# Query tiles of the first batch through DRAM: attention and mixture layer, one core

## The reference, cut to what matters

```python
x = x + xattn(layernorm(x), ctx, ctx, q_norm_w, k_norm_w, w_out)   # x (4, 512, 512), ctx (4, 512, 128)
x = x + ffn(layernorm(x), ...)

def xattn(q, k, v, ...):                  # 16 query heads of width 32, 4 key heads, 4 query heads a key head
    q, k = rms_norm(q), rms_norm(k)
    q, k = rope(q), rope(k)
    scores = einsum(q, k) / sqrt(32), causal mask, softmax
    return (scores @ v).reshape(B, T, 512) @ w_out.T

def ffn(x, ...):                          # 128 experts as mixtures of 8 bases, top 4, and a shared part
    basis = silu(x @ w_gate) * (x @ w_up)                            # (tokens, 8, 256)
    mixed = per expert, basis weighed with mix(amplitudes); times w_down; summed with the router's weights
    return mixed + silu(x @ shared_gate) * (x @ shared_up) @ shared_down
```

## Time and profile before

| | us |
|---|---|
| median of 3 runs | 840.32 |
| lowest, highest | 839.88, 840.95 |
| profiled execution, first to last instruction | 839.9 |
| TensorE busy in it | 783.9 (93%) |
| VectorE, ScalarE, GpSimd busy | 664.1, 578.4, 525.0 |

### The profile page before, as it was taken

How to read it: one execution, slowest core, us unless ns; L and a number is a source line. 1 busy time by engine, 2 the same in 40 slices (tenths; PEclk the granted TensorE clock), 3 DMA queues, 4 the chain that set the end, 5 groups by cost and what they waited for, 6 DMA issues and landing times. The chain is left out here.

```text
span 839.9 us, 15209 instructions
## 1 busy us (share of the span) xinstructions
PE 783.9 (93%) x4180; PEld 610.7 (73%) x4180; DVE 664.1 (79%) x1635; ACT 578.4 (69%) x1413; POOL 525.0 (63%) x687
## 2 busy tenths in 40 slices
PE   3768899899999999989999999989999999999998
PEld 2645566677877777767777788767777787788876
DVE  7657678789888878889888878779878787688774
ACT  3867787677777767778777677678777775654542
POOL 5547457986488646997477834997566624661561
PEclk9969699999999999999999999999999999999999
DMA  8222144445445445744454435545445435454550
GB/s 300 104 68 80 28 130 166 142 143 168 155 161 170 149 156 174 230 144 129 147 192 161 153 119 182 168 143 174 148 162 169 152 114 173 158 184 130 205 192 26
DMA packets 57051, 127.02 MB, mean 151 GB/s; under 512 B 10920, under 2 KB 28040, under 8 KB 56968
## 3 DMA queue, kind: packets, MB, share of 16 engines
q1 hardware_dynamic: 56968, 126.04, 45.5%
HBM read 107.55 MB, written 4.46 MB: 133 GB/s over the span
## 5 line engine op out<-in xcount | busy, mean ns | idle before, releaser
L1602 PE MATMUL u<-w_h,t_h 128*128 128x512 f32 x640 | 258.9, 404 | 5.3 <-POOL w_l L889 2.7
L1259 DVE TENSOR_TENSOR w_l<-w_raw,w_h 128x512 fp32r<-128x512 f32 x288 | 253.4, 907 | 0.2 <-ACT w_h L931 0.2
L1602 PE MATMUL u<-w_l,t_h 128*128 128x512 f32 x640 | 251.2, 393 | 0.0
L1602 PE MATMUL u<-w_h,t_l 128*128 128x512 f32 x640 | 251.0, 392 | 0.0
L931 ACT ACTIVATE w_h<-w_raw 128x512 fp32r<-128x512 f32 x384 | 219.2, 621 | 13.4 <-DMA w_raw<-in_w_units 13.1
L889 POOL TENSOR_TENSOR w_l<-w_raw,w_h 128x512 fp32r<-128x512 f32 x96 | 138.2, 1440 | 98.3 <-ACT w_h L931 97.5
L965 ACT ACTIVATE scores<-scores,mx 128x384 f32<-128x384 f32 (+1 forms) x224 | 128.4, 573 | 78.3 <-DVE mx L1203 77.1
L1203 DVE CUSTOM_DVE_ANT_0 scores<-s,mask_qk 128x384 f32<-128x384 f32 (+1 forms) x224 | 112.3, 503 | 45.5 <-PE s L1480 44.8
L1602 PEld LDWEIGHTS u<-w_h,t_h 128*128 128x128 f32 x640 | 120.9, 189 | 33.7 <-issue 6.1
L897 POOL TENSOR_TENSOR macc<-macc,gb 128x256 f32<-128x256 f32 x112 | 103.5, 926 | 66.4 <-DVE gb L1360 66.0
L1602 PEld LDWEIGHTS u<-w_h,t_l 128*128 128x128 f32 x640 | 120.5, 188 | 27.1
(11 more groups left out here) (151 smaller groups left out, 1196.1 us busy)
## 6 DMA issues: line engine op xcount, KB each, us to landing
w_raw<-in_w_units SPq DMA_DIRECT2D x160, 512.0 KB, 4.2
w_raw<-in_w_out_t SPq DMA_DIRECT2D x16, 512.0 KB, 5.0
w_raw<-in_shared_w_down SPq DMA_DIRECT2D x16, 512.0 KB, 4.5
q_st<-turned_h SPq DMA_DIRECT2D x232, 32.0 KB, 1.9
out<-x SPq DMA_DIRECT2D x16, 256.0 KB, 2.2
q_st<-turned_l SPq DMA_DIRECT2D x116, 32.0 KB, 1.9
x<-in_x SPq DMA_DIRECT2D x3, 1024.0 KB, 8.9
k_st<-turned_h SPq DMA_DIRECT2D x48, 32.0 KB, 1.9
```

Source lines behind the costliest of these rows:

```text
L1259: e.tensor_tensor(w_l[:, i % WR, k, :], w_raw[:, i % WR, k, :], f32(w_h[:, i % WR, k, :]), ALU.subtract).then_inc(s_wl, 1)
L1602: last = e.matmul(u_bank[n % 2][:], t[:, k, cols], ww[:, i % WR, k, :], start=(k == 0 and m == 0), stop=(k == KC - 1 and m == 2))
```

## The change

Four more tiles are named in the tuple that selects the path through DRAM:

```diff
-THROUGH_DRAM = (5,)
+THROUGH_DRAM = (5, 6, 7, 8, 9)
```

## The result

| | before | after |
|---|---|---|
| median, us | 840.15 (4 runs) | 853.07 (851.58 to 853.58, 4 runs) |
| ratio to before | | 1.0140, 95% interval 1.0125 to 1.0156 |
| profiled execution, first to last instruction | 839.9 | 851.7 |

The changed kernel is 1.4% slower, about 11.8 us by the ratio. I forecast 848.8, with 851.8 as the upper end: the direction and the path were right, the size was too small.

A forecast was written before the change was run, and what follows sets the result against it. It took TensorE, busy 93% of the span, as the bound, with early delays paid at the end. 7.5 - 0.4 + 1.4 = 8.5 us over 839.9, plus 0.4 for the timed median, gave 848.8 us; range 842.6 to 851.8.

The forecast's parts named there:

- Which tile is exposed, and that it is paid in full: Span 4's first product: of the four tiles only tile 6 is exposed, its delay handed on to the end; +7.5 us.
- The engines of the load: High part's load of tile 6: two copies outermost, so 2 of 16 engines; chance 0.66.
- Rival 1: Tile 6's load uses all engines: first product at 54.9, time 843.2 us; chance 0.20.
- The size of the load: Tile 6's high part: 128 KB per engine at 24 GB/s, 5.45 us; store to product 10.95 us.
- Tile 7: Span 5's first product waits 2.45 us, less a swallowed 1.06 us wait at L1460: net +1.4 us.
- head 1's wait: TensorE's 0.40 us wait before 53.51 for tile 6's head 1 goes, since all heads are there: -0.4 us.
- Tile 8: Span 6's queries: loaded until about 82, needed at 85.9, so hidden with 3.9 us of cover.
- Tile 9: Slot 34: its stores delay chunk and maxima rows by 2.4 us; rows 0.4 late, covered; cost 0, at most 2.4.
- SP's saved issues: SP's queue: 48 issues become 16, some 20 us less, but SP then waits for others; worth 0.
- The clock: TensorE's 1.2 GHz stretches: a second stall at 69 may slow some products; left at 0, 1 us in the range.

The follow-up runs named there:

- Experiment 9: Kernel before, with 8 padding stores of 32 KB issued on SP ahead of tile 6's copies: 843.85 us, ratio 1.0031 to before.
- experiment 5: Changed kernel, with the high part loaded by two loads of 32 partitions instead of one two-copy load: 845.90 us, ratio 1.0055 to before.
- experiment 11: Changed kernel with 128-row stores and three 32-partition loads per tile, tile 6 back on its copies: 838.04 us, ratio 0.9969 to before.
- experiments 7: Kernel before with the 128-row store for tile 5, and key loads of heads 2 and 3 behind tile 6's copies: 838.48 us, ratio 0.9975.

## Why the prediction was wrong, step by step

- **Which tile is exposed, and that it is paid in full:** right for tile 6. Its loss is 8.7 us alone, for a first product that is 8.9 us later (62.02 in its profile, 18.90 behind tile 5's store). Experiment 9 hands on 2.6 of 3.77.
- **The engines of the load:** right. The step from "4 heads outermost, a quarter of the engines" to "2 copies outermost, two engines" fits the share of 0.12, and experiment 5 shows that the shape was the cost. Rival 1 is out.
- **The size of the load, the term that failed.** The chain from tile 6's store to the product was put at 10.95 us and measured 12.29 (11.99 to 12.35 in the three experiments with the same chain). The store's 3.46 was exact (49.75 to 53.21). The rest, from the load's issue, was put at 7.5 and took 8.8. Two engines at 43 GB/s move 256 KB in 6.1 us, where I had taken 24 GB/s for each from a stretch with all 16 busy and got 5.45. The store's own row had the better figure: 92 GB/s at a share of 0.27 is 21 GB/s for each engine, and 128 KB at that rate take the 6.1 us. The other 0.7 lies before the first and behind the last byte, where I had read fixed parts off a store and put them on a load. Nothing moves from 61.00 on, and the product starts at 62.04: 1.0 us, where I had 0.5.
- **Tile 7, the same term again.** Tile 7 was put at +1.4 and head 1's wait at -0.4, together 1.0; from the first product to L1460 the runs showed 2.9. Tile 7's chain was 12.79 us: the same load, and a store that released SP after 4.02 us, not 3.46. Since tile 7's store stands behind span 4's first product, I knew that each us of error counts nearly twice. The errors of the two chains, 1.3 and 1.8, make nearly all of what was missing at L1460: 11.75 us behind, where the forecast has 8.5. I had allowed the chain only 0.7 in the range.
- **Head 1's wait:** hardly given back (0.1 of 0.4), because the turn of tile 8 is paced by GpSimd.
- **Tile 8:** hidden, right. **Tile 9:** the rows were to be 0.4 us late and covered. They were 2.4 late and mostly covered. They were issued as late as forecast, but from their issue to L1504 it was 7.5 us (94.44 to 101.96), and my 0.4 needs 5.3 (rows issued at 89.5, landed at 94.7). Tiles 8 and 9 alone cost 1.0, which I had at 0.
- **SP's saved issues:** put at 0, and nothing shows (experiment 11).
- **The clock:** I left it at 0. In the profile after, TensorE had 1.2 GHz for half as long around 100 us, and the kernel is 1.5 us less behind past that stretch than ahead of it. Whether that is due to the change isn't settled. The change isn't needed for it: two kernels that keep the path of the kernel before for these tiles, those of experiments 7 and 9, had the short stretch too (one window of each, in this order):

```profile
85.15:91.97 6.82, 5.42 (x19) 0.50 0.22 56
90.30:97.13 6.83, 5.37 (x19) 0.50 0.20 53
```

By the runs the sum is 8.7 for tile 6, 2.3 for tile 7 behind it, and 0.8 for tiles 8 and 9: 11.8 us. The parts are differences of nested kernels and so must add up; what bears them out is that the profiles show 8.8 and 2.9 for the first two, and that tiles 8 and 9 alone cost 1.0.

## What to carry to other kernels

In this kernel the outermost dimension of a DMA set its time before its bytes did: with 4 heads outermost, or 2 broadcast copies, most engines stood idle. The same store with 128 rows outermost released SP 1.5 us earlier, and the same load in parts of 32 rows ended its wait 5 us earlier. So write down the outermost sizes of source and destination for each DMA on the path. Before a transfer is moved to another path, count the chain up to the first instruction that needs it. And where the next transfer's store stands behind the product that the last one delays, carry the chain's uncertainty twice.

## What the runs showed of the hardware

- A store of 128 KB to DRAM took 3.46 us to release its waiter at a DMA share of 0.27, and 1.97 us at 0.78. The Trainium skill ("DMA: Bandwidth & Descriptors", "Anatomy of one DMA") has a formula, 2.0 us and the bytes over 436 GB/s, fitted to DMAs that GpSimd issues; my estimate by it is 2.3 us. These stores were issued by SyncE, so the formula, which rival 1 of the prediction uses too, isn't made for them; the second time is 0.3 us below it, the first 1.2 us above.
- A broadcast source read twice by one DMA ran at 43 GB/s and a share of 0.12; as two DMAs, with the low part's beside them, the loads ran at 219 GB/s and a share of 0.78.
- The first 40 us of the same code differed by up to 1.9 us between profiled executions (tile 5's store at 41.59 to 43.45, thirteen profiles). A difference of that size between two profiles is no finding by itself.
